# Attention and mixture-of-experts block on one core: at a step's end, the raw projection copy ahead of the rotated tile's high part

## What is computed

```python
x = x + layernorm(attention(layernorm(x)))
x = x + layernorm(ffn(layernorm(x)))
```

```python
q = rotate(x @ Wq); k = rotate(x @ Wk); v = x @ Wv
probs = softmax(causal(q @ k.T / 8))
out = (probs @ v) @ Wo
```

## Time and profile before

| | us |
|---|---|
| median of 3 runs | 1385.63 |
| lowest, highest | 1384.83, 1387.22 |
| the profiled execution, its own time | 1387.9 |
| its span | 1386.0 |

### The profile page before, as it was taken

How to read it: one execution, slowest core, us unless ns; L and a number is a source line. 1 busy time by engine, 2 the same in 40 slices (tenths; PEclk the granted TensorE clock), 3 DMA queues, 4 the chain that set the end, 5 groups by cost and what they waited for, 6 DMA issues and landing times.

```text
span 1386.0 us, 31149 instructions
## 1 busy us (share of the span) xinstructions
PE 1282.0 (93%) x10504; PEld 947.4 (68%) x10504; DVE 966.3 (70%) x1953; ACT 781.8 (56%) x1725; POOL 464.8 (34%) x481
## 2 busy tenths in 40 slices
PE   2799999999999999999999999999999899999996
PEld 2577777778777776877777668777777665555553
DVE  6577777774777778577777784777777466677755
ACT  3466666654666666466666664666666343444444
POOL 1242444332434434134334332334342022333222
PEclk7799999999999999999999999999999999999999
DMA  4612112120212120112111111111110011121220
GB/s 134 182 40 72 61 49 68 40 66 28 70 49 76 34 73 32 54 48 77 38 64 62 48 54 43 40 66 68 42 68 17 1 62 61 62 76 72 98 100 23
DMA packets 80452, 83.70 MB, mean 60 GB/s; under 512 B 40176, under 2 KB 62832, under 8 KB 79216
## 3 DMA queue, kind: packets, MB, share of 16 engines
q1 hardware_dynamic: 79168, 82.21, 17.6%
q10 hardware_dynamic: 1200, 0.39, 0.1%
HBM read 23.99 MB, written 2.23 MB: 19 GB/s over the span
## 4 chain that ended last, share of the span: by engine, by line
PE 66%; DVE 14%; ACT 9%; issue 8%; SPq 2%; DMA 1%; POOL 1%; ACTq 0%; DVEq 0%; POOLq 0%
PE rows L483 16%; PE o_out L532 14%; PE turn L502 9%; DVE neg_max L1151 5%; ACT probs L774 4%; PE rows L486 3%; PE proj_bank L502 3%; PE o_out L693 2%; PE o_out L442 2%; PE rows L425 2%; PE proj_bank L442 2%; PE rows L427 1%; PE rows L426 1%; PE proj_bank L425 1%; PE proj_bank L427 1%
## 5 line engine op out<-in xcount | busy, mean ns | idle before, releaser
L774 ACT ACTIVATE probs<-rows,neg_max 128x768 f32<-128x768 f32 (+7 forms) x512 | 375.0, 737 | 249.2 <-DVE neg_max L1151 244.1
L1151 DVE TENSOR_REDUCE neg_max<-rows 128x1 f32<-128x768 f32 (+7 forms) x512 | 363.4, 752 | 117.5 <-PE rows L486 117.5
L532 PE MATMUL o_out<-probsT,v_g 128*64 128x128 f32 (+1 forms) x3328 | 280.1, 319 | 0.7 <-DVE probsT L1165 0.7
L532 PEld LDWEIGHTS o_out<-probsT,v_g 128*64 128x64 f32 x3328 | 202.9, 137 | 68.7 <-issue 19.9
L502 PE MATMUL turn<-cf,probs 128*128 128x128 f32 x1792 | 239.5, 274 | 1.3 <-DVE probsT L1165 1.1
L483 PE MATMUL rows<-kk,qh 64*128 64x512 f32 (+2 forms) x768 | 164.9, 425 | 54.6 <-ACT probs L774 41.2
L783 ACT ACTIVATE probsT<-turn 128x512 f32<-128x512 f32 x256 | 152.7, 596 | 109.8 <-PE turn L502 106.4
L502 PEld LDWEIGHTS turn<-cf,probs 128*128 128x128 f32 x1792 | 192.2, 141 | 1.9 <-DVE probsT L1165 1.3
L997 POOL COPY inv_wide<-inv_sum 128x256 f32<-128x256 f32 x128 | 52.2, 408 | 393.6 <-DVE inv_sum L1157 377.9
L1165 DVE COPY probsT<-turn 128x512 f32<-128x512 f32 x256 | 174.7, 682 | 1.4 <-PE turn L502 1.1
L483 PEld LDWEIGHTS rows<-kk,qh 64*128 64x128 f32 x768 | 72.2, 184 | 132.2 <-ACT probs L774 93.5
(11 more groups left out here) (166 smaller groups left out, 1871.4 us busy)
## 6 DMA issues: line engine op xcount, KB each, us to landing
turned<-raw SPq DMA_DIRECT2D x188, 128.0 KB, 2.0
kk<-kk SPq DMA_DIRECT2D x16, 512.0 KB, 2.9
kl<-kl SPq DMA_DIRECT2D x16, 512.0 KB, 3.7
v_g<-v_all SPq DMA_DIRECT2D x32, 256.0 KB, 2.9
probsT<-scratch SPq DMA_DIRECT2D x4, 2048.0 KB, 7.8
attnT<-scratch SPq DMA_DIRECT2D x4, 2048.0 KB, 7.0
slab_a<-w_qk SPq DMA_DIRECT2D x15, 256.0 KB, 2.5
xm<-in_x SPq DMA_DIRECT2D x4, 512.0 KB, 5.2
```

The costliest lines, as they stand in the source:

```text
L532: ins = mm(dst, v_g[p][:, t, :], x, start=t == 0, stop=t == big_w - 1)
L774: A(probs[:, s % 2, q * 128:q * 128 + width], rows[h][:, 0:width], ACT.Exp, bias=neg_max[:, s % 2, item:item + 1], accum_out=exp_sum[:, s ...
L1151: V.tensor_reduce(neg_max[:, s % 2, item:item + 1], rows[h][:, 0:width], AX_X, ALU.max, negate=True).then_inc(max_ready, 1)
```

## The change

In ScalarE's `step` the loop over `keep_raw` moves up, in front of the loop over `keep_high`. All else stays, the waits of both included.

```diff
@@ -831,6 +831,8 @@
                 if first and s == 1 and b:
                     keep_out(b - 1, 0, proj_bank)
                     keep_out(b - 1, 1, o_out)
+                for ahead, k in rope_plan(b, s, 0, last):
+                    keep_raw(b, g + ahead, k, proj_bank)
                 for ahead, k in rope_plan(b, s, 1, last):
                     keep_high(b, g + ahead, k)
                 if last and b == B - 1 and s >= 3:
@@ -841,8 +843,6 @@
                     A(w_high_at[s - 3], w_up[:, (s - 3) * HALF:(s - 3) * HALF + HALF], ACT.Copy).then_inc(wx_high, 1)
                 if last and s == 2:
                     keep_tokens(b + 1, 1, proj_bank)
-                for ahead, k in rope_plan(b, s, 0, last):
-                    keep_raw(b, g + ahead, k, proj_bank)
                 if first and s == 0:
                     keep_values(b)
```

## The result

| | before | with the change |
|---|---|---|
| median, us | 1387.22 (5 runs) | 1425.39 (5 runs) |
| lowest, highest | 1384.83, 1389.38 | 1424.69, 1427.19 |
| ratio | | 1.0275, 95% interval 1.0264 to 1.0286 |
| span of the profiled execution | 1386.0 | 1425.3 |

The kernel is 38.2 us slower; the forecast was +36, and 1421.6 in a range from 1410 to 1432. (The runs of before now include those made beside the changed kernel, so their median is 1.6 us above the one of the table ahead of the prediction.)

The account below looks back on a forecast made before the run. TensorE was taken to bound the kernel. 61 pairs x 0.64 us made 39 us, less 3.4 for exceptions, say +36 us, giving 1421.6 us against the median of 1385.63; range 1410 to 1432.

Parts of the forecast that it names:

- What bounds: TensorE, busy 93% of the span; ScalarE's high part to exponentials has 0.39 us to spare at the end of step 5.
- The order alone: ScalarE's high part starts 0.49 us later behind the raw copy; beyond the slack, 0.10 or 0.11 us reaches TensorE.
- The collision: GpSimd's cosine product overlaps VectorE's subtraction, which ends 0.55 us behind it, 1.03 later than before.
- The strict lock: VectorE's whole 0.69 us subtraction would follow GpSimd's product: 8.5 us more, about 1430.
- Per pair: TensorE loses 0.64 us in steps 1, 4 and 5, 0.65 in step 6; 61 pairs make 39 us.
- No cost elsewhere: Only steps 1, 4, 5 and 6 change order; the earlier raw copy gains nothing in all but the first pair.
- The exceptions: First raw-copy and high-part pair, -2.1 us, and two step ends with a batch's output addition, -1.3: 3.4 us off.
- The two heads behind an output addition: Where a batch's output addition holds VectorE, a later high part costs nothing: -1.3 us.
- The first pair: TensorE works during its 6.04 us wait; the small block starts 1.5 us sooner instead of losing 0.64: -2.1 us.
- Order alone: Rival: GpSimd and VectorE do not hold each other up; 0.10 us per pair, +4 us, 1390; chance 0.09.
- Slack that covers it: Rival: exponentials have over 0.5 us to spare, no collision; 60 pairs cost nothing, 1380 to 1384 us; chance 0.03.
- Piling up: Rival: delays of a step add up to the next, each pair costing up to 1.03 us: 1445 us; chance 0.04.

Follow-up runs that it names:

- the line of six kernels: Change; change with GpSimd's product waiting; kernel before with extra GpSimd product (320, 640 columns), copy, fill: 1425.39; 1395.14; 1391.91, 1428.11, 1393.13, 1387.42 us.
- the collision taken away: On top of the change, GpSimd's cosine product waits until VectorE's subtraction of the step is done: 1395.14 us, ratio 1.0049 to the kernel before.
- the single steps: Kernel before with the raw copy first in step 4 alone, 1397.37 us (ratio 1.0073), or in step 6 alone, 1395.95 us (ratio 1.0059).

## Why the prediction was right

- *What bounds.* The path from the high part over subtraction, maxima and exponentials to the small block, with 0.39 us to spare, is confirmed by the line of six kernels.
- *The order alone.* The high part moved by 0.48 to 0.50 us (forecast 0.49) and leaves 0.10, as forecast. At the head of step 5 it leaves 0.16 where I had 0.10 too: the raw copy starts 0.11 us behind the projection, not 0.05.
- *The collision.* Forecast: the product 0.41 ahead of the subtraction, which ends 0.55 behind it and 1.03 later than before. Measured: 0.41, 0.56, 1.04. The strict lock, with the whole 0.69 behind the product, would have given 0.14 more in each pair; the four kernels whose collision is shown above have 0.54 to 0.56.
- *Per pair.* 0.64 or 0.65 forecast, 0.65, 0.64 and 0.64 measured in the heads of 6, 7 and 2. In step 5 it was 0.70 against 0.64: the one term per pair that was too small, about 1 us in sum.
- *No cost elsewhere.* The heads of 0, 1 and 4 did not change (median 0.00). The earlier raw copy gave nothing, as forecast, since nothing waits for its sum in a regular step.
- *The exceptions.* The two heads behind an output addition grew by 0.00 and -0.21, as forecast. The first pair, for which I took 2.1 us off the sum, did not deliver: this step of the prediction was wrong. The small block came 0.57 us sooner in the changed kernel, and the next one 0.71 later, because TensorE's slow stretch moved onto the step between them. That the miss stays small is owed to there being only one such pair. It and step 5 are the 2 to 3 us by which the forecast was short.
- *Rivals.* Order alone was worked out at +4 and measured at +7.4 with the collision taken away; as an account of the change it is refuted, since the change costs 38. Slack that covers it: refuted. Piling up: refuted, by the single steps.

## What to carry to other kernels

When two instructions change places on an engine that is half idle, look at what each of them releases on the others: the order by itself cost 7 us here, but the copy moved up also released GpSimd's product into the moment of VectorE's subtraction, and that cost 31. Before moving anything, note for each path the slack in front of the engine that bounds, and check whether shifted work of GpSimd and VectorE will overlap. If it does, a wait that lets the critical one go first can take the collision away; here it cost nothing, since GpSimd had time.

## What the runs showed of the hardware

- A subtraction with both inputs in SBUF that is issued beside a running GpSimd instruction which reads SBUF ends 0.54 to 0.56 us after that one, whatever its length (0.40, 0.88, 0.94, 1.09, 1.55 us). One input on GpSimd's side is enough. Beside a GpSimd fill, which only writes, it runs undisturbed in 0.69.
- Alone the subtraction takes 0.69 us, so being held costs it 0.14 us less than the rest of the GpSimd instruction.
- It works both ways: GpSimd's product of 512 columns, issued behind a held subtraction, took 1.54 us in place of 1.09.
- GpSimd's length does not follow the columns in proportion, nor the columns alone. The product of two constant tables took 0.88 us for 320 columns and 1.55 for 640; a line through these two gives 1.28 for 512. Its sums of two tensors took that (line 1013: a mean of 1.27 us for 512 columns), but its products with one constant table 1.09 (line 1008). Why these differ was not tested. A copy took 0.40 us for 256 columns and 0.94 for 896. Scaling from one row misjudged both lengths, of the products and of the copy.
- TensorE's granted clock was 0.50 behind its wait of 6.04 us in the first pair, and 0.52 behind the wait of 2.27 us in the run that swaps only this pair. At this level the turning of six blocks took 1.49 us in place of 0.83.
